# Four layers on one core: banded weights loaded ready-made, linear attention interleaved over images, attention's rounding and copies moved

## What is computed

```python
qkv = conv1x1(x, w_qkv)
agg = conv1x1(conv5x5(qkv, w_dw, groups=3 * td), w_pw, groups=3 * HEADS)
ms = concatenate([qkv, agg], axis=1)        # heads of 8 channels: q, k, v
q, k = relu(q), relu(k); v = pad(v, ones)
kv = einsum('bgnd,bgne->bgde', k, v)        # a sum over all pixels of an image
out = einsum('bgnd,bgde->bgne', q, kv)
out = out[..., :-1] / (out[..., -1:] + EPS)
return conv1x1(out, w_proj)
```

## Time and profile before

| | us |
|---|---|
| median of three runs | 9316.44 (9316.26 to 9318.12) |
| the profiled execution, its own time | 9307.04 |
| its span, first to last instruction | 9305.5 |
| window attention in it | 1447 |
| grouped convolution | 982 |
| linear attention | 928 |
| mean granted TensorE clock | 0.944 |

### The profile page before, as it was taken

How to read it: one execution, slowest core, us unless ns; L and a number is a source line. 1 busy time by engine, 2 the same in 40 slices (tenths; PEclk the granted TensorE clock), 3 DMA queues, 4 the chain that set the end, 5 groups by cost and what they waited for, 6 DMA issues and landing times. The chain is left out here.

```text
span 9305.5 us, 159969 instructions
## 1 busy us (share of the span) xinstructions
PE 8011.6 (86%) x55850; PEld 6805.6 (73%) x55850; DVE 5823.2 (63%) x9258; ACT 3539.4 (38%) x6969; POOL 4537.8 (49%) x2070
## 2 busy tenths in 40 slices
PE   3888886759996777569999999999999999938999
PEld 2666664649996565458888888888888888836777
DVE  3555555454442343479888989888888889842110
ACT  3444444313332222234445545444445545530000
POOL 2444443003332000047778878777777878831111
PEclk9999998879998888889999999999999999969999
DMA  5111113846775455410000000000000000052111
GB/s 195 52 52 61 53 52 129 295 143 144 146 146 142 173 160 149 159 70 17 6 17 17 17 17 17 17 13 17 6 17 17 17 17 17 8 164 105 63 61 55
DMA packets 435343, 703.76 MB, mean 76 GB/s; under 512 B 273645, under 2 KB 280301, under 8 KB 425390
## 3 DMA queue, kind: packets, MB, share of 16 engines
q1 hardware_dynamic: 389550, 502.28, 17.4%
q0 software_dynamic: 38656, 176.79, 6.3%
q10 hardware_dynamic: 6528, 16.78, 0.6%
HBM read 422.53 MB, written 273.22 MB: 75 GB/s over the span
## 5 line engine op out<-in xcount | busy, mean ns | idle before, releaser
L1705 POOL TENSOR_TENSOR e_ev<-e_se,e_v 128x2048 f32<-128x2048 f32 (+1 forms) x896 | 3311.6, 3714 | 916.6 <-ACT e_se L1671 916.6
L1671 ACT ACTIVATE e_se<-e_stage 128x512 f32<-128x512 f32 x3136 | 1878.2, 599 | 2082.4 <-PE e_stage L1545 2056.3
L1795 DVE SCALAR_TENSOR_TENSOR e_stage<-e_k,e_rl,e_qp 128x512 f32<-128x512 f32 x3136 | 2302.6, 746 | 318.6 <-ACT e_se L1671 279.2
L1552 PE MATMUL e_pv_sum<-e_ident,e_ev 128*128 128x128 f32 x12544 | 1874.1, 273 | 38.1 <-issue 37.6
L1552 PE MATMUL e_pe_sum<-e_ident,e_se 128*128 128x128 f32 x12544 | 1878.0, 272 | 0.1
L1552 PEld LDWEIGHTS e_pe_sum<-e_ident,e_se 128*128 128x128 f32 x12544 | 1556.3, 139 | 227.3 <-issue 2.0
L1552 PEld LDWEIGHTS e_pv_sum<-e_ident,e_ev 128*128 128x128 f32 x12544 | 1487.9, 141 | 264.8 <-issue 211.4
L1545 PE MATMUL e_stage<-e_top,e_minus 128*128 128x512 f32 x3136 | 1508.7, 481 | 45.3 <-DVE e_stage L1795 43.9
L363 POOL TENSOR_TENSOR a_pr<-a_pr,a_rden 128x480 f32<-128x480 f32 x512 | 493.9, 985 | 683.0 <-DVE a_rden L583 683.0
L852 POOL DMA_DIRECT2D agg<-c_ot x384 | 329.0, 862 | 950.9 <-DVE c_ot L910 839.1
L886 PE MATMUL c_pa<-c_x_high,c_w_high 128*128 128x320 f32 x1920 | 602.3, 314 | 111.4 <-DVE c_w_low L965 111.4
(11 more groups left out here) (154 smaller groups left out, 12357.7 us busy)
## 6 DMA issues: line engine op xcount, KB each, us to landing
xn<-n_xnp POOLq DMA_DIRECT2D x32, 2450.0 KB, 14.9
qkv<-b_ot SPq DMA_DIRECT2D x120, 512.0 KB, 5.8
c_xt<-qkv SPq DMA_DIRECT2D x384, 160.0 KB, 4.3
agg<-c_ot POOLq DMA_DIRECT2D x384, 160.0 KB, 3.0
n_xt<-x SPq DMA_DIRECT2D x24, 2048.0 KB, 11.8
a_xb<-xn SPq DMA_DIRECT2D x32, 840.0 KB, 6.2
e_xb<-xn SPq DMA_DIRECT2D x16, 1540.0 KB, 7.0
f_xb<-xn SPq DMA_DIRECT2D x32, 700.0 KB, 6.0
```

The costliest lines, as they stand in the source:

```text
L1552: last = nc.tensor.matmul(acc[:, c * PART:(c + 1) * PART], lhsT=src[:, c * PART:(c + 1) * PART], rhs=ident[:], is_transpose=True, start=j ...
L1671: nc.scalar.activation(se[(t * K2 + o) % NSE][:, i], stage[:, bank_of(t, j), :], ACT.Exp)\
L1705: nc.gpsimd.tensor_tensor(split(ev[(t * NG2 + g) % NEV][:, 0:size]), split(se[(t * K2 + o) % NSE][:, i:i + size]), window(v[h], h, u, o, i ...
L1795: nc.vector.scalar_tensor_tensor(rows(stage[:, bank_of(t, j), :]), win, rl[:, h, o:o + 1], rows(qp[:]), ALU.add, ALU.mult).then_inc(multip ...
```

## The change

Four things, in the order of the program:

- In window attention ScalarE rounds a band in two halves, in steps 6 and 7 of the band two ahead of it in the same buffer, instead of both in step 0 of the band before it. GpSimd makes the first half of `a_x_low` in step 7 behind that step's normalising and the second half in step 0 of the next band, also behind the normalising; the masks move to step 2. SyncE's loop is written so that a band and its masks are fetched before the exchange of the other buffer's results.
- VectorE's step becomes: maximum, inversion, addition, copy of the values, copies of the turned weights.
- The grouped convolution loads its bands ready-made, 128 x 7680 float32 (3.93 MB) in two transfers, in place of the taps and the masks. The 75 instructions that built them are gone.
- Linear attention is written out for four images. Keys and values come in half tiles through five buffers each, all queries on SyncE's queue; a turned block is 512 pixels on one bank for keys and one for values, the ratios have two banks, the turned-back block one, the projection two. Image 0's keys and values are summed first; then each of the 32 steps of image b also turns and sums one block of image b + 1; the last image has its steps alone. ScalarE clips the second half of an image's queries in steps 5, 6, 11 and 12 and the first half of the next image's in steps 21, 22, 27 and 28.

```diff
-        SPLIT_AT = 0
+        ROUND_AT = (6, 7)
+        SPLIT_AT = (7, 0)
+        MASKS_AT = 2
...
-                    load_band(n, u)
-
-                    sp.wait_ge(masks_rounded, n * 2 + u - 1)
-                    load_masks(n, u)
-                    store(n - 1, u)
-                    sp.wait_ge(out_stored[u], n * 16)
-                    load_rest(n, u)
+            load_ahead(1, 0)
+            with sp.Fori(1, ALL - 1) as n:
+                load_ahead(n, 1)
+                exchange(n, 0)
+                load_ahead(n + 1, 0)
+                exchange(n, 1)
+            load_ahead(ALL - 1, 1)
+            for u in range(2):
+                exchange(ALL - 1, u)
             for u in range(2):
                 store(ALL - 1, u)
...
             def step(n, P, first=False, final=False):
                 band, at = divmod(P, BP)
-                if at == SPLIT_AT and not (final and band == 1):
-                    split(n, band + 1)
                 normalise(n, P)
-                if at == SPLIT_AT and not (final and band == 1):
+                if at == SPLIT_AT[0] and not final:
+                    split(n, band + 2, 0)
+                if at == SPLIT_AT[1] and not (final and band == 1):
+                    split(n, band + 1, 1)
+                if at == MASKS_AT and not (final and band == 1):
                     round_masks(n, band + 1)
 
-            split(0, 0)
+            for h in range(HALVES):
+                split(0, 0, h)
             round_masks(0, 0)
+            split(0, 1, 0)
...
-                    round_band(n, band + 1)
-
-            round_band(0, 0)
+                if at in ROUND_AT and not final:
+                    round_band(n, band + 2, ROUND_AT.index(at))
+
+            for u in range(2):
+                for h in range(HALVES):
...
 
-            def lagging(n, P, first=False):
+            def step(n, P, first=False, final=False):
+                t, s = divmod(P, 2)
+                if P < PT:
+                    maximum(n, P)
                 if P - 1 < PT and (P >= 1 or not first):
                     invert(n, P - 1)
+                if s == 1 and (P >= O_LAG + 1 or not first):
+                    add(n, (P - O_LAG - 1) // 2)
+                if s == 1 and not (final and t + 1 >= NT):
+                    copy_v(n, t + 1)
                 if P - LAG < PT and (P >= LAG or not first):
                     copy_turned(n, P - LAG, first)
...
-            sp.dma_start(rm[:], row_masks).then_inc(consts_in, 16)
+            sp.dma_start(pw[:].rearrange("p g o -> p (g o)"),
+                         bass.AP(tensor=w_pw.tensor, offset=w_pw.offset, ap=[w_pw.ap[0], [0, BLK], w_pw.ap[1]])).then_inc(consts_in, 16)
+            half = GROUPS // 2
+            for i in range(2):
...
-            nc.vector.memset(band[:], 0.0).then_inc(band_step, 1)
-            dve.wait_ge(band_step, 1)
-            done = 1
-
-            for dy in range(K1):
-                for y in range(BLK):
-                    j = y + dy - K1 // 2
-                    if 0 <= j < BLK:
-                        to = band[:, :, :, y]
-                        nc.vector.scalar_tensor_tensor(to, dw[:, :, dy, :], rm[:, j:j + 1], to, ALU.mult, ALU.add)\
-                            .then_inc(band_step, 1)
-                        done += 1
-
-                dve.wait_ge(band_step, done)
-
             def prepare(n, u):
...
 
-def row_masks():
-    return (np.arange(PART)[:, None] % BLK == np.arange(BLK)[None]).astype(np.float32)
+def banded(w_dw):
+
+    taps = w_dw.reshape(GROUPS, G8, K1, K1).transpose(1, 0, 2, 3)
+    out = np.zeros((G8, BLK, GROUPS, K1, BLK), np.float32)
+    for y in range(BLK):
+        for dy in range(K1):
+            j = y + dy - K1 // 2
+            if 0 <= j < BLK:
...
+            for g in range(NH - 1):
+                load_keys(g)
+            sp.dma_start(wp[:], w_proj_t.rearrange("(s p) o -> p s o", p=PART)).then_inc(wp_in, 16)
+            for g in range(NHALF + HALF_STEPS):
+                if g + NH - 1 < NHALF:
+                    load_keys(g + NH - 1)
+                if g >= HALF_STEPS // 2:
+                    half, at = divmod(g - HALF_STEPS // 2, HALF_STEPS // 2)
+                    if half < 2 * B:
+                        for t in Q_AT_STEP.get(at, ()):
+                            load_queries(*divmod(half, 2), t)
 
         @block.gpsimd
...
+            for j in range(NQ):
+                turn(j)
+                if j:
+                    accumulate(j - 1)
+            pe.wait_ge(wp_in, 16)
+            for b in range(B):
+                for i in range(NI):
+                    if i or not b:
+                        ratio(b, i)
+                    j = (b + 1) * NQ + i
+                    if b + 1 < B:
                         turn(j)
...
+            for j in range(NQ):
+                copy_keys(j)
+            for st in range(ST):
+                clip_queries(0, 0, st)
+            for b in range(B):
                 for i in range(NI):
+                    if b + 1 < B:
+                        copy_keys((b + 1) * NQ + i)
+                    if i in CLIP_AT:
+                        clip_queries(b, 1, CLIP_AT[i])
+                    if b + 1 < B and i - NI // 2 in CLIP_AT:
+                        clip_queries(b + 1, 0, CLIP_AT[i - NI // 2])
...
+                            add(b - 1, NPC - 1)
+                    divide(b, i)
+                    if i and b + 1 < B:
+                        copy_values(j)
+                        if i % QPT == 0:
+                            mask_sums(j // QPT - 1)
+                    if i and i % ST == 0:
+                        add(b, i // ST - 1)
+            add(B - 1, NPC - 1)
+
 
 
```

More of the change, by code:

```diff
@@ L521, in round_band @@
                     act.wait_ge(v_projected, (n * 2 + u - 1) * TILES)
[L522 to L524 removed]
+                nc.scalar.activation(tiled(x_high[u % 2], h), areas(xb[u % 2], h), ACT.Copy).then_inc(x_high_ready, 1)
             def copy_qk(n, u, part):
@@ L1028, in linear_attention @@
         sums_masked = sem("sums_masked")
-        ratio_parts = [sem(f"ratio_parts{v}") for v in range(2)]
+        rated = sem("rated")
         den_steps = sem("den_steps")
@@ new lines, in load_queries @@
+            def load_queries(b, v, t):
+                if b:
+                    sp.wait_ge(rated, (b - 1) * NI + (v + 1) * (NI // 2))
+                for run in HALF_RUNS[v]:
+                    sp.dma_start(qt[:, t, pixels(run)], heads_of(b, t, 0, run)).then_inc(q_in[v][t // 2], 16)
+            for g in range(NH - 1):
[9 more added lines that the diff above has]
+                            load_queries(*divmod(half, 2), t)
@@ new lines, in load @@
+            def load(k):
+                if k >= 2:
+                    pool.wait_ge(stored[k % 2], k // 2 * 16)
+                pool.dma_start(xr[k % 2][:], of_chunk(x_in, *divmod(k, NPC))).then_inc(x_loaded[k % 2], 16)
+            load(0)
+            load(1)
+            for k in range(B * NPC):
+                pool.wait_ge(added, (k + 1) * HALVES)
+                pool.dma_start(of_chunk(x_out, *divmod(k, NPC)), xr[k % 2][:]).then_inc(stored[k % 2], 16)
+                if k + 2 < B * NPC:
+                    load(k + 2)
@@ new lines, in accumulate @@
+            def accumulate(j):
+                tile, k = divmod(j, QPT)
+                pe.wait_ge(keys_copied, j + 1)
+                pe.wait_ge(values_copied, j + 1)
+                if k == 0 and tile:
+                    pe.wait_ge(sums_masked, tile * 2)
+                for e in range(SUB):
+                    last = nc.tensor.matmul(pkv[:, 0:PART + 1], lhsT=kvp[j % NKV][:, e, 0:PART],
+                                            rhs=kvp[j % NKV][:, e, PART:2 * PART + 1],
+                                            start=k == 0 and e == 0, stop=k == QPT - 1 and e == SUB - 1)
+                last.then_inc(summed, 1)
@@ new lines, in ratio @@
+            def ratio(b, i):
+                c, st = divmod(i, ST)
+                if c % (NPC // 2) == 0:
+                    pe.wait_ge(q_positive, b * (2 * ST) + (2 * c // NPC) * ST + st + 1)
+                if c == 0:
+                    pe.wait_ge(sums_masked, (b * ST + st + 1) * 2)
+                if b or i:
+                    pe.wait_ge(attended, b * NI + i)
+                for s in range(SUB):
+                    queries = qt[:, st, c * PC + s * PART:c * PC + (s + 1) * PART]
+                    last = nc.tensor.matmul(ratios[:, s // SPB, s % SPB, :], lhsT=queries, rhs=kvm[b % 2][:, st],
+                                            start=True, stop=True)
+                last.then_inc(rated, 1)
@@ new lines, in back, with project @@
+            def back(b, i):
+                pe.wait_ge(attended, b * NI + i + 1)
+                if b or i:
+                    pe.wait_ge(att_copied, b * NI + i)
+                for s in range(SUB):
+                    last = nc.tensor.transpose(att_bank[:, s * PART:(s + 1) * PART], attp[i % 2][:, s], ident[:])
```

(10 more changed lines are left out.)

362 lines of the change are left out of this document (144 added, 218 removed).

## The result

The changed kernel takes **8994.47 us** (median of 4, 8987.96 to 8995.97), the kernel before 9316.35: a ratio of 0.9655, 95% interval 0.9638 to 0.9672. The forecast was 9015. The profiled execution went from 9305.5 us of span to 8986.0.

| | before | after | gain in the stage | forecast |
|---|---|---|---|---|
| attention's last addition | 1556.6 | 1479.0 | 77.6 | 103 |
| convolution's last product | 2939.4 | 2783.3 | 78.5 | 73 |
| linear attention's last addition | 3872.5 | 3547.0 | 169.4 | 125 |
| the end | 9305.5 | 8986.0 | -6.0 | 0 |

What follows compares the result with a forecast made beforehand. Attention was taken as bound by TensorE with holes, linear attention by something taking turns with TensorE. Attention 103, convolution 73 and linear attention 125 make 301 us off 9307: 9006 profiled, 9015 median; range 8925 to 9105.

Steps and rivals of the forecast that it cites:

- The copy of the values: Window attention, odd steps: copying right behind the addition starts TensorE's projection 1.36 us sooner, 62 times, 84 us.
- The cost that it feared: Window attention: turned copies 0.7 us later, costed at nothing; without cover at most 43 us over 62 steps.
- The rounding: Window attention: wait for `a_x_low` stays, ending 0.6 us later; turning gets faster, winning 0.6 us a band, 19 in all.
- so the turning that needs it takes 1.91 us: Window attention before: turning said to wait for step 0's normalising behind the halves; eight turnings otherwise take 1.04 us.
- Attention's high end of 189: Window attention: both waits, 160.9 us, and 31 x 0.9 of turning gone; as a rival 8929 us, 6%.
- Convolution: Grouped convolution: loading ready-made bands instead of building them on VectorE saves 73 us (67 to 77), first `c_wm` at 1992.
- Steps of linear attention: Linear attention: 4.96 us for a step that also sums the next image, 3.4 us in the last image.
- the division isn't on the path: Linear attention: VectorE's 1.7 us division hidden in interleaved steps; the rival with it on the path: 9158 us, 5%.
- The loads: Linear attention: SyncE's queue at 145 GB/s sets step 5 of image 2; stage ends at 3748, saving 125 us.
- u: Linear attention: time to load 2.1 MB, taken as 14.5 us; the stage's end is 3342 + 28u.
- the first rival: Linear attention: loads at 207 GB/s throughout, TensorE bounds all three images, 161 to 188 us saved, 8965; 14%.
- The 145 GB/s: Linear attention: load rate taken for SyncE's queue, from four old stretches together at 148 GB/s.

Runs made afterwards that it cites:

- the order alone: Kernel before with only VectorE's new order in window attention (values copied ahead of turned weights, inversion ahead of addition): 9216.2 us, ratio 0.9895.
- the convolution's run: Kernel before with only the ready-made bands of the grouped convolution: 9231.19 us, ratio 0.9905.

## Why the prediction was right, and where not

1. **The copy of the values: right, too small.** It said 1.36 of each 1.54 us. All of it went, 95.6 us, and 5 more in the wait for `a_x_low` and the clock around it: 100.8 by the run with the order alone. The cost that it feared, turned blocks 0.7 us late, is nil. (With the old attention's end 7 us apart from trace to trace, the 5 are within what the traces can tell.)
2. **The rounding: wrong in sign.** The order and the later end of the wait were right (2.47 us idle where 2.06 were). The failed step is "so the turning that needs it takes 1.91 us": it read the length of an instruction as waiting for the normalising. The rows of the clock show the lower level before and after, and after, the turning takes 1.91 us with its operand ready 4.7 us earlier. So nothing was won at the turning. Behind the longer pause the slow stretches are longer too, on average (3.5 us a band before, 4.2 after); that the longer pause makes them so is argued, not shown. In place of 19 us won, 23.4 lost. Together 77 in place of 103.
3. **Attention's high end of 189** was out of reach of this change for the reason given, two normalisings and two halves ahead of the projection. But the clock is in none of the sum's terms for attention: with it the wait was worth 135 to 140 us, not its 77.
4. **Convolution: right.** 77 for 73, at the upper end of its range: `c_wm` starts at 1984 in the old kernel's time, not 1992.
5. **Steps of linear attention: right**, 4.91 for 4.96, 3.33 for 3.4; the division isn't on the path while images overlap.
6. **The loads: the term that was mis-sized.** The mechanism held: some 27 MB until image 0's first queries were all there, then a wait for queries in step 5. But u was 10.3 us (2.1 MB at 204 GB/s) up to there, 11.5 up to step 5 (45.9 us for 4u), and 12.5 beside GpSimd's chunks (3063 to 3173, the row below), not 14.5: below the 13.25 (159 / 12) from which loads bound an image. Of the 44 us too little, the first queries gave 12 (2926.5 where the forecast, less what was gained ahead, has 2939), the way to step 5 another 12, and the images that loads no longer bound 20. It is the first rival that came near, whose 161 to 188 us hold the 169, though its 207 GB/s throughout did not come.

```profile
q1 hardware_dynamic: 7222, 18.52, 44.9%
```

The 145 GB/s were near the mean of the four stretches of the old kernel (148), whose queue stopped and restarted six times. The traces show what goes with that: after it has stood empty within the stage, the queue runs at 130 to 137 GB/s for 10 to 60 us, then at 207. The kernel before, in image 2 (3471 to 3511), slow throughout:

```profile
DMA packets 1803, 5.49 MB, mean 137 GB/s; under 512 B 111, under 2 KB 111, under 8 KB 1801
q1 hardware_dynamic: 1801, 5.45, 51.5%
```

The share is that of the fast stretches, so each packet took half as long again. The new queue runs on for 220 us, past the end of image 0's loads, without a stop, and stops four times later, each with 20 to 30 us of the slow rate behind it. Standing empty is not all of it: at the stage's start in the changed kernel the queue is fast 10 us after its first load (2803 to 2813, 202 GB/s):

```profile
q1 hardware_dynamic: 962, 2.02, 52.0%
```

That the total was within 21 us of the forecast is luck in good part. Errors stand against each other: attention 25 too high, convolution 5 and linear attention 44 too low, and 6 lost behind them; and within attention the copy 17 too low and the rounding 42 too high.

## What to carry to other kernels

Before a long instruction is explained by a wait, read the granted clock of its stretch: TensorE's pauses of 2.5 us cost 1.7 times their length here (134.7 us for 77.4 of waiting), and moving one half of `a_x_low` ahead of one normalising won most of it back. Read a load rate by stretches and by what the queue did before each, not as a mean: here it was 204 GB/s while image 0 was loaded and 168 beside GpSimd's chunks, though the mean over images 1 to 3, with its stops, is 147, close to the 145 forecast. That mean holds stops of the queue in which TensorE went on at 4.9 us a step (3183 to 3193, for one).

## What was not expected of the hardware

- TensorE's waits for `a_x_low`, once a band, had a stretch at the lower clock with them, begun in the wait or within some 2 us behind it, in 27 of 31 bands of the kernel before (waits of 1.95 to 2.09 us, the first 4.90), 30 of 31 with VectorE's order alone (1.82 to 1.95, the first 4.90) and 31 of 31 in the changed kernel (2.45 to 3.06). The stretches were nearly all 3.4 or 6.8 us long. Waits of 0.57 to 0.69 us never had one (30 waits, the second half ahead of the normalising), those of 1.54 us in odd steps had one twice in 62. So in these traces the length of the one wait doesn't settle it, and what else does stays open.
- A queue's rate after a stop, 130 against 207 GB/s at the same share of engines and nearly the same size of packets (3.0 and 2.9 KB). What makes it so stays open: it isn't the turns of keys and values, nor the tensors' places as far as the convolution's run moved them. On 16 engines no slow stretch was seen, but there every packet is as slow as in it (267 GB/s at a share of 1.04).
- 16 engines moved 1.3 times what 8 did (267 against 206 GB/s), not twice. Why isn't known.
